# A front without queries, and a lag of two between gate and down products, in a gated cross-attention and mixture-of-experts layer on one core

## The chip, the cores and the metric

The kernel runs on one NeuronCore of a Trainium2 chip. The metric is the device time of one execution in microseconds. A core has five engines that run side by side, each through its own list of instructions: PE (TensorE, matrix products), DVE (VectorE), ACT (ScalarE), POOL (GpSimd) and SP (SyncE, which here only issues transfers). They wait for each other by semaphores.

## The reference, cut to what matters

```python
# x: (4, 256, 256), ctx: (4, 256, 64)
p    = layernorm(x)                                    # no gamma
kv   = ctx @ W_k.T + b_k
out  = einsum('bij,bjd->bid', p, kv)                   # queries
sim  = einsum('bid,bjd->bij', out, kv) / 16
sim  = (sim - mean) * rsqrt(var + 1e-6) * ln_gamma + ln_beta
x    = x + tanh(g_xattn) * softmax(sim)
h    = layernorm(x)                                    # 1024 tokens
s    = sigmoid(h @ gate_weight.T)                      # 16 experts, 4 groups
# two best groups by s + bias, four best experts of these, weights s/sum * 2.5
out  = sum_e w[t,e] * (silu(h @ gate_w[e].T) * (h @ up_w[e].T)) @ down_w[e].T
out += (silu(h @ sh_gate.T) * (h @ sh_up.T)) @ sh_down.T
x    = x + tanh(g_ffn) * out
```

## The kernel before

**Batches, halves, steps.** The 1024 tokens lie in 8 tiles of 128, two to a batch, four to a half of 512. Every expert is computed for every token and weighted with zero where it wasn't chosen. The shared expert counts as two of 128 columns, so each half has NF = 18 steps, 36 in all; step k is expert k of the first half, or k - 18 of the second. Precision comes from splitting: each fp32 operand becomes a high part (fp32r) and the rest as a low part, and three products stand for one (high times high, high times low, low times high).

**A step.** PE does the gate product (6 of 512 columns, L782), the up product (6 of 512) and, for the step before (lag of one), the down product (12 of 256, L826, L828, L834) into accumulators in PSUM banks 4 and 5 (first half) or 6 and 7. ACT takes the silu of the gate (L386), and makes the high parts of weights two steps ahead (high_gu) and of the down weights one ahead (high_d, both L327). POOL subtracts to get the low parts (L284). DVE multiplies by the expert's weight per token (L535, from a row that is broadcast by a transfer), then by up: act_hi (L553), the same product in fp32 (L556), and act_lo, the difference (L561). The first two routed experts, steps 2 and 3 (WEIGHTED_LAST), get their weight last, because the routing is late then: step 2's row comes by transposes on PE (first_row, L769), step 3's by the transfer. Steps 18 and 19 are shared again.

**What waits for what.** gate(k) waits for act_done of step k - 2 (L804), up(k) for actlo_done of k - 2 (L813), down(k - 1) for the parts of k - 1 (L822, L830).

**The front.** For each batch: statistics of x (L458 to L464), the power -1/2 on POOL (L278), the normalised x on DVE or ACT, its transposes on PE (L712), the context's projections kv and kvT (L700, L705), the query product (L721), the similarity (L729), its statistics, centring (L487), scaling (L495), maximum (L499), exponential on ACT (L363), residual (L514), statistics of the new x, hidden rows (L470), their transposes and high and low parts (L368, L524). Batches 0 and 1 are done before the steps; all four similarities are made before step 0 and batches 2 and 3 finish on DVE between steps 2 and 12. Products of zeros (keep_warm, L852) fill PE's waits.

**The routing.** route (L752) makes the logits transposed, logitT is copied by ACT, route_back (L760) transposes them, DVE adds the parts (L571), ACT takes an exponential (L378), and DVE does score_groups, rank_groups, mask_groups and pick_experts (L573 to L627): some 40 small instructions with waits between them. The order of all engines is written out by hand; each_step names which pieces come after which step. In before the routing of the first half is spread: scores ahead of step 0's parts, ranks after step 0, picks after step 1.

**Loads.** SP issues x in four pieces, then the weights of eight steps (384 KB each), later one slice and one row a step. ACT's queue issues the context, the vectors and the router's weights.

## Time and profile before

| | us |
|---|---|
| median of 3 runs | 195.62 |
| lowest, highest | 194.97, 199.32 |
| the profiled execution's own time | 194.61 |
| its span, first to last instruction | 192.8 |
| PE busy | 183.1 (95%) |
| DVE busy | 147.1 (76%) |
| ACT busy | 81.2 (42%) |
| POOL busy | 83.0 (43%) |

The span is what the trace covers; 1.8 us of the execution's time lie around it. A busy engine is one with an instruction in flight. Products are pipelined, so a row of a product can be longer than the distance to the next. The start of a row and the distance between starts say more than its length.

### The profile page before, as it was taken

The numbers are of one execution on the slowest core, as the hardware profiler recorded it, in microseconds if no ns is written. First come the engines' busy times: TensorE is split into PE (matmuls) and PEld (weight loads), VectorE is DVE, ScalarE is ACT, GpSimd is POOL, SyncE is SP. The second block draws the span as 40 slices with busy tenths as digits, with TensorE's granted clock in tenths as the row PEclk, the third lists the DMA queues.
The fourth block names the chain that finished last, engine by engine and source line by source line (L and its number), as shares of the span: only waits on it lengthen the run. The fifth ranks groups of instructions, "written<-read, shape, count | busy, mean of one in ns | idle before, by whom it ended". The sixth has DMA issues, their size and how long they took to land.

```text
span 192.8 us, 3265 instructions
## 1 busy us (share of the span) xinstructions
PE 183.1 (95%) x1003; PEld 151.9 (79%) x1003; DVE 147.1 (76%) x332; ACT 81.2 (42%) x160; POOL 83.0 (43%) x101
## 2 busy tenths in 40 slices
PE   6999799969899999999999989999999999999993
PEld 5665457858788888888788868888888888888882
DVE  1759988989899699998469999885666665566664
ACT  2449725523248833435457333434334343433220
POOL 2352162822841755553345543454444555444410
PEclk9999999999999999999999999999999999999999
DMA  5967200002785555541221000312211221221403
GB/s 145 344 212 217 76 0 0 0 0 57 235 205 183 150 141 163 161 139 58 54 54 54 0 3 9 109 57 74 80 60 54 54 54 60 74 78 60 143 20 112
DMA packets 10297, 18.08 MB, mean 94 GB/s; under 512 B 1773, under 2 KB 3821, under 8 KB 10286
## 3 DMA queue, kind: packets, MB, share of 16 engines
q1 hardware_dynamic: 9504, 17.11, 29.4%
q10 hardware_dynamic: 782, 0.83, 1.8%
q8 instruction: 6, 0.10, 0.2%
q14 instruction: 5, 0.04, 0.1%
HBM read 16.82 MB, written 1.11 MB: 93 GB/s over the span
## 4 chain that ended last, share of the span: by engine, by line
PE 67%; DVE 20%; DMA 6%; issue 2%; POOL 1%; ACT 1%; DVEq 0%; SPq 0%; POOLq 0%
PE bank L782 41%; PE bank L834 8%; PE bank L826 7%; PE bank L828 7%; DMA xs<-x_in 3%; DVE act_hi L553 2%; DVE bank L556 2%; DVE act_lo L561 2%; DMA w_row<-weight_rows 2%; DVE stats L458 1%; POOL rstd L278 1%; PE bank L712 1%; DMA weight_rows<-w_blk 1%; DVE beats L597 1%; PE bank L752 1%
## 5 line engine op out<-in xcount | busy, mean ns | idle before, releaser
L284 POOL TENSOR_TENSOR w_lo<-w_raw,w_hi 128x256 fp32r<-128x256 f32 (+1 forms) x72 | 72.4, 1024 | 76.7 <-ACT w_hi L327 75.6
L327 ACT CAST w_hi<-w_raw 128x256 fp32r<-128x256 f32 (+2 forms) x72 | 36.5, 513 | 56.4 <-PE bank L834 30.6
L782 PE MATMUL bank<-hT_hi,w_hi 128*128 128x512 f32 x142 | 56.5, 398 | 0.0
L782 PE MATMUL bank<-hT_lo,w_hi 128*128 128x512 f32 x142 | 56.0, 395 | 0.0
L782 PE MATMUL bank<-hT_hi,w_lo 128*128 128x512 f32 x142 | 44.7, 396 | 0.0
L535 DVE TENSOR_TENSOR weighted<-bank,w_row 128x512 f32<-128x512 f32 x30 | 20.7, 691 | 25.6 <-ACT bank L386 24.5
L826 PE MATMUL bank<-w_hi,act_hi 128*128 128x256 f32 x144 | 36.0, 283 | 1.8 <-DVE act_hi L553 1.8
L828 PE MATMUL bank<-w_lo,act_hi 128*128 128x256 f32 x144 | 35.8, 281 | 0.0
L782 PEld LDWEIGHTS bank<-hT_hi,w_lo 128*128 128x128 f32 x142 | 26.7, 188 | 6.3
L782 PEld LDWEIGHTS bank<-hT_hi,w_hi 128*128 128x128 f32 x142 | 26.8, 189 | 5.1
L826 PEld LDWEIGHTS bank<-w_hi,act_hi 128*128 128x128 f32 x144 | 27.2, 189 | 4.3 <-issue 2.8
L782 PEld LDWEIGHTS bank<-hT_lo,w_hi 128*128 128x128 f32 x142 | 26.8, 189 | 4.8
L386 ACT ACTIVATE bank<-bank 128x512 f32<-128x512 f32 x30 | 17.5, 582 | 26.4 <-PE bank L782 26.4
L828 PEld LDWEIGHTS bank<-w_lo,act_hi 128*128 128x128 f32 x144 | 27.2, 189 | 1.4
L561 DVE TENSOR_TENSOR act_lo<-bank,act_hi 128x512 fp32r<-128x512 f32 (+1 forms) x37 | 25.0, 677 | 3.6
L553 DVE TENSOR_TENSOR act_hi<-bank,weighted 128x512 fp32r<-128x512 f32 (+1 forms) x36 | 24.2, 675 | 2.8 <-DVE weighted L535 0.9
L834 PE MATMUL bank<-w_hi,act_lo 128*128 128x256 f32 x144 | 23.8, 287 | 1.0 <-DVE act_lo L561 0.7
L556 DVE TENSOR_TENSOR bank<-bank,weighted 128x512 f32<-128x512 f32 (+1 forms) x36 | 24.2, 675 | 0.0
L834 PEld LDWEIGHTS bank<-w_hi,act_lo 128*128 128x128 f32 x144 | 19.7, 190 | 2.2 <-DVE act_lo L561 2.2
L278 POOL TENSOR_TENSOR rstd<-var_eps,half_neg 128x2 f32<-128x2 f32 x12 | 8.7, 721 | 20.5 <-DVE var_eps L464 20.4
L852 PE MATMUL bank<-zeros 128*128 128x512 f32 x25 | 9.1, 508 | 1.5 <-DVE zeros L636 1.5
L852 PEld LDWEIGHTS bank<-zeros 128*128 128x128 f32 x25 | 5.6, 243 | 3.6 <-DVE zeros L636 1.5
(100 smaller groups left out, 133.2 us busy)
## 6 DMA issues: line engine op xcount, KB each, us to landing
w_row<-weight_rows SPq DMA_DIRECT2D x31, 256.0 KB, 3.2
w_raw<-w_in SPq DMA_DIRECT2D x18, 384.0 KB, 3.9
xs<-x_in SPq DMA_DIRECT2D x4, 256.0 KB, 5.9
out<-x SPq DMA_DIRECT2D x2, 256.0 KB, 3.5
cw<-ctxw_in ACTq DMA_DIRECT2D x1, 276.2 KB
vec<-vecs_in ACTq DMA_DIRECT2D x1, 265.0 KB, 5.6
out<-x SPq DMA_DIRECT2D x2, 128.0 KB, 1.8
out<-x ACTq DMA_DIRECT2D x2, 128.0 KB, 1.8
```

The lines of the kernel that those rows point to most:

```text
L284: nc.gpsimd.tensor_tensor(w_lo[:, par, cols], w_raw[:, bass.ds(n, 1), cols].rearrange("p o c -> p (o c)"), w_hi[:, par, cols].bitcast(F32) ...
L327: nc.scalar.copy(w_hi[:, par, cols], w_raw[:, bass.ds(n, 1), cols].rearrange("p o c -> p (o c)"))\
L386: nc.scalar.activation(gate_ps[par][:, :] if routed else weighted[:, par, :], gate_ps[par][:, :], ACT.Silu).then_inc(silu_done, 1)
L535: nc.vector.tensor_tensor(weighted[:, par, :], gate_ps[par][:, :], w_row[:, par, :], ALU.mult)\
L553: nc.vector.tensor_tensor(act_hi[:, par, toks], row[:, toks], weighted[:, par, toks], ALU.mult)\
L556: nc.vector.tensor_tensor(up_ps[par][:, toks], row[:, toks], weighted[:, par, toks], ALU.mult)\
L561: nc.vector.tensor_tensor(act_lo[:, par, toks], up_ps[par][:, toks], act_hi[:, par, toks].bitcast(F32), ALU.subtract).then_inc(actlo_done, 1)
L782: last = nc.tensor.matmul(dst, w[:, par, w0 + c * P:w0 + (c + 1) * P], m, start=i == 0, stop=i == len(parts) - 1, skip_group_check=True)
L826: nc.tensor.matmul(acc, act_hi[:, par, own], w_hi[:, par, rows], start=start and t % 2 == 0, stop=False, skip_group_check=True)
L828: nc.tensor.matmul(acc, act_hi[:, par, own], w_lo[:, par, rows], start=False, stop=False, skip_group_check=True)
L834: last = nc.tensor.matmul(acc, act_lo[:, par, own], w_hi[:, par, rows], start=False, stop=True, skip_group_check=True)
L852: last = nc.tensor.matmul(spare[:, :], zeros[:, 0:P], zeros[:], start=True, stop=True)
```

## The change

**Front.** The queries go. With the augmented context c (64 columns and a one), similarity is x c' M c, where M is the square of the key weights. So: squared() makes W'W (65x65) from W with its bias as a 65th column; the context of each batch is centred over its positions (times 256, so that no division is needed), which makes the similarity's row means zero; offset(b) is a product of one column that becomes the 65th column of the batch's square; projected(b) gives u (65x256); gathered(b) gives r (65x256) from context rows and x transposed, which now comes ready from the host as a fifth array; similarity(b) is r times u. Normalising x falls away, since the layer norm after it removes scale and mean: only the epsilon is corrected, by row_eps from x's variance. For batches 0 and 1 a second product with u times minus gamma (similarity_gamma) gives the scaled logits; ACT multiplies them by the root, and one DVE instruction adds minus beta and takes the minimum. Batches 2 and 3 keep scaling, logits and maximum on DVE.

**Loads.** SP's queue takes nearly all, in the order of need; ACT's has the key weights and the context rows of batch 0.

**Lag of two.** down(k - 2) stands in step k. Activation parts and down weights have three buffers. gate(k) waits for the weighting of k - 2 (weighted_done, or the silu where there is none) instead of act_done. In steps 2 and 3 DVE splits: weighted_late(k) inside the step, late_parts(k) later. The loops are unrolled.

**Moved.** The low parts of down weights are made for step k, not k + 1. Steps 0 and 1 are done by batches: gate and up for batch 0 of both before hidden(1). Similarities 2 and 3 stand among them. All of the first routing stands after step 1 on DVE; the router's exponential on ACT is after step 1 too.

```diff
 def each_step(eng, step, between):
-    straight(0, NF + 2)
-    loop(NF + 2, 2 * NF - 2)
-    straight(2 * NF - 2, 2 * NF)
+    for k in range(2 * NF):
+        step(k, k % 2)
+        for piece in between.get(k, ()):
+            piece()
 # SP
-            for b in range(B):
-                sp.dma_start(xs[...], x_v[...]).then_inc(x_in[b], 16)
-            ahead = 8
-            for n in range(ahead):
...
+            load_context(0, 1, cT0_in)
+            load_xT(0)
+            sp.dma_start(gamma_key[:], ...).then_inc(gamma_in, 16)
+            load_x(0)
+            load_context(1, 2, cT1_in)
+            load_xT(1)
+            load_rows(1, 2, rows1_in)
+            load_x(1)
+            sp.dma_start(vec[:], ...).then_inc(vec_in, 16)
+            load_slice(0, 0)
+            load_slice(1, 1)
+            load_context(2, B, cT_in)
+            load_xT(2)
+            load_xT(3)
+            load_rows(2, B, rows_in)
+            sp.dma_start(gw[:], ...).then_inc(gw_in, 16)
+            load_x(2)
+            load_x(3)
 # PE
             def gate_up(k, par, half):
                 pe.wait_ge(hi_gu, k + 1)
-                    pe.wait_ge(act_done, k - 1)
+                if k >= 2:
+                    if shared_or_late(k - 2):
+                        pe.wait_ge(silu_done, k - 1)
+                    else:
+                        pe.wait_ge(weighted_done, weighted_count(k - 2))
...
             def step(k, par):
-                if first == 1:
-                    pe.wait_ge(score_ready, 1)
-                    down(k - 1, 1 - par, int(first - 1 >= NF), first - 1 in (0, NF))
+                gate_up(k, par, k // NF)
+                if k >= 2:
+                    if k % NF == 2:
+                        pe.wait_ge(score_ready, k // NF + 1)
+                    down(k - 2)
 # ACT
-            table_change = {6: ..., 15: lambda: logit_exp(1)}
+            table_change = {7: lambda: (softmax_exp(2), softmax_exp(3)), 16: lambda: logit_exp(1)}
 # DVE
+            def sim_logits_negative(b):
+                for i, t in enumerate(tiles(b)):
+                    dve.wait_ge(scaled_read, 2 * b + i + 1)
+                    nc.vector.tensor_tensor_reduce(logit[:, t, :], scaled[:, t, :], beta_neg[:], 1.0, BIG, ALU.add, ALU.min,
+                                                   neg_max[:, t:t + 1]).then_inc(max_ready[b], 1)
...
             each_step(dve, step, {
-                0: [rank_groups, mask_groups],
-                1: [lambda: pick_experts(0)],
-                2: [lambda: sim_stats(3), lambda: sim_centre(3)],
...
+                1: [lambda: add_logits(0), lambda: score_groups(0), rank_groups, mask_groups, lambda: pick_experts(0)],
+                2: [lambda: sim_stats(2), lambda: sim_scale(2)],
+                3: [lambda: late_parts(2), lambda: x_stats(3), lambda: sim_stats(3), lambda: late_parts(3)],
+                4: [lambda: sim_scale(3)],
+                5: [lambda: sim_logits(2, 5)],
+                6: [lambda: sim_logits(3, 6)],
...
```

DVE's list around the first routing before: scores, then step 0's three parts, then the ranks (L593 on).

```order
L583 TENSOR_TENSOR pairs<-choice 128x16
L584 TENSOR_REDUCE gscore<-pairs 128x16
L553 TENSOR_TENSOR act_hi<-bank,weighted 128x512
L556 TENSOR_TENSOR bank<-bank,weighted 128x512
L561 TENSOR_TENSOR act_lo<-bank,act_hi 128x512
L593 TENSOR_TENSOR beats<-gscore 128x64
L594 TENSOR_TENSOR ties<-gscore 128x64
```

The same place of the changed kernel: the end of the routing (w_blk is what SP writes out for the row transfers), then step 2's and 3's late weighting (L588), batch 2's statistics and the late parts of step 2.

```order
L696 TENSOR_TENSOR w_tok<-pick_w,w_rec 128x4x16
L700 STREAM_TRANSPOSE w_blk<-w_tok 128x64
L588 TENSOR_TENSOR weighted<-bank,weighted 128x512
L488 BN_STATS stats<-bank 128x6 x2
L491 BN_AGGR meanvar<-stats 128x2 x2
L524 TENSOR_TENSOR var_eps<-meanvar,row_eps 128x2
L530 TENSOR_TENSOR scaled<-bank,vec 128x256 x2
L588 TENSOR_TENSOR weighted<-bank,weighted 128x512
L603 TENSOR_TENSOR act_hi<-bank,weighted 128x512
L604 TENSOR_TENSOR weighted<-bank,weighted 128x512
L606 TENSOR_TENSOR act_lo<-weighted,act_hi 128x512
```

The parts of steps 0 and 1 stand ahead of the whole routing now, and the parts of step 2 behind it and behind batch 2's statistics.

PE's list around the first early products before: zero products, both batches' hidden transposes (L712), the gate of batch 0, then the route.

```order
L852 MATMUL bank<-zeros 128x512 x6
L712 MATMUL bank<-ident,ln 128x128 x8
L795 MATMUL bank<-hT_hi,w_hi 128x256 x2
L795 MATMUL bank<-hT_hi,w_lo 128x256 x2
L795 MATMUL bank<-hT_lo,w_hi 128x256 x2
L752 MATMUL bank<-hT_hi,gw_parts 32x512 x2
```

And of the changed kernel, from early_up(1, 0) to the route (L873); L826 is the hidden transposes of batch 1, L840 a similarity, L804 a projected context.

```order
L916 MATMUL bank<-hT_lo,w_hi 128x256 x2
L826 MATMUL bank<-ident,hid 128x128 x4
L789 MATMUL bank<-ctx_sum,square 65x1
L840 MATMUL bank<-uT,rT 128x256 x2
L804 MATMUL bank<-cT_mid,square 65x256
L916 MATMUL bank<-hT_hi,w_hi 128x256 x2
L916 MATMUL bank<-hT_hi,w_lo 128x256 x2
L916 MATMUL bank<-hT_lo,w_hi 128x256 x2
L873 MATMUL bank<-hT_hi,gw_parts 32x512 x2
```

The transposes of batch 1 come behind four products with batch 0 (L916), and a similarity and a projection stand between them and the route.

## Rows read from the trace of the kernel before

**Rows 1.** The page: busy shares; granted clock of PE in 40 slices.

```profile
PE 183.1 (95%) x1003; PEld 151.9 (79%) x1003; DVE 147.1 (76%) x332; ACT 81.2 (42%) x160; POOL 83.0 (43%) x101
...
PEclk9999999999999999999999999999999999999999
```

**Rows 2.** Waits of PE: who waited for whom, us in total, times, longest.

```profile
PE bank L826 <- DVE act_hi L553: 1.8, 2, 1.4
...
PE bank L834 <- DVE act_lo L561: 0.7, 1, 0.7
```

**Rows 3.** The chain that ended last: start us, us, what.

```profile
61.51 2.79 PE bank L782 x12
...
65.73 2.79 PE bank L782 x12
...
97.45 3.02 PE bank L782 x12
...
115.94 2.79 PE bank L782 x12
```

**Rows 4.** Timeline of DVE, front: start us, us, instruction [idle before].

```profile
5.25 0.75 DVE L458 BATCH_NORM_STATS2 stats<-xs 128x6 f32<-128x256 f32 x2 [3.85 <-DMA xs<-x_in]
...
9.55 0.74 DVE L458 BATCH_NORM_STATS2 stats<-xs 128x6 f32<-128x256 f32 x2
...
10.62 0.75 DVE L458 BATCH_NORM_STATS2 stats<-xs 128x6 f32<-128x256 f32 x2
...
13.81 0.76 DVE L458 BATCH_NORM_STATS2 stats<-bank 128x6 f32<-128x256 f32 x2 [2.02 <-PE bank L729]
...
27.46 0.69 DVE L524 TENSOR_TENSOR hT_lo<-bank,hT_hi 128x512 fp32r<-128x512 f32 x1 [0.15 <-ACT hT_hi L368]
```

**Rows 5.** Timelines of PE in five stretches, the last with its weight loads.

```profile
4.62 1.41 PE L852 MATMUL bank<-zeros 128*128 128x512 f32 x3
...
7.81 0.97 PE L852 MATMUL bank<-zeros 128*128 128x512 f32 x3
...
10.53 1.08 PE L721 MATMUL bank<-lnT,kv 128*64 128x256 f32 x4
...
57.12 0.40 PE L782 MATMUL bank<-hT_hi,w_hi 128*128 128x512 f32 x1
...
188.38 0.30 PEld L834 LDWEIGHTS bank<-w_hi,act_lo 128*128 128x128 f32 x2 [0.20 <-DVE act_lo L561]
```

**Rows 6.** Groups by line: count | busy us, mean ns | idle before.

```profile
L284 POOL TENSOR_TENSOR w_lo<-w_raw,w_hi 128x256 fp32r<-128x256 f32 (+1 forms) x72 | 72.4, 1024 | 76.7 <-ACT w_hi L327 75.6
...
L278 POOL TENSOR_TENSOR rstd<-var_eps,half_neg 128x2 f32<-128x2 f32 x12 | 8.7, 721 | 20.5 <-DVE var_eps L464 20.4
...
L363 ACT ACTIVATE prob<-logit,neg_max 128x256 f32<-128x256 f32 x8 | 4.0, 500 | 1.3 <-DVE neg_max L499 1.3
...
L514 DVE SCALAR_TENSOR_TENSOR x<-prob,attn_scale,xs 128x256 f32<-128x256 f32 x7 | 3.1, 480 | 0.1
...
L470 DVE TENSOR_SCALAR ln<-x,meanvar,rstd 128x256 f32<-128x256 f32 x8 | 2.8, 406 | 0.3 <-POOL rstd L278 0.3
```

**Rows 7.** Timeline around the first routing, ACT and DVE.

```profile
31.45 0.26 ACT L378 ACTIVATE inv_score<-route_logit 128x64 f32<-128x64 f32 x1 [0.92 <-DVE route_logit L571]
...
31.73 1.28 ACT L386 ACT_TABLE_LOAD   x1
31.74 0.20 DVE L577 TENSOR_SCALAR inv_score<-inv_score 128x64 f32<-128x64 f32 x1 [0.32 <-ACT inv_score L378]
...
36.46 1.20 DVE L596 TENSOR_TENSOR ties<-ties,before 128x64 f32<-128x64 f32 x1
...
43.68 0.24 DVE L626 STREAM_TRANSPOSE w_blk<-w_tok 128x64 f32<-128x64 f32 x1
```

**Rows 8.** The chain: the weights' way out and the first row's way back.

```profile
43.96 2.06 DMA weight_rows<-w_blk
46.03 3.21 DMA w_row<-weight_rows
```

More of the change, by code:

```diff
@@ new lines, in _ @@
+                9: [lambda: x1_stats(2), lambda: residual(3)],
+                10: [lambda: x1_stats(3)],
+                11: [lambda: normalise(2, 2, 7, x1, hid, hid_ready)],
+                12: [lambda: normalise(2, 3, 8, x1, hid, hid_ready)],
+                13: [lambda: hidden_low(2), lambda: hidden_low(3)],
+                15: [lambda: add_logits(1)],
+                16: [lambda: score_groups(1), rank_groups],
+                17: [mask_groups, lambda: pick_experts(1)],
+                NF + 1: [lambda: result(0)],
@@ L883, in _ @@
-            keep_warm(6, bank[5])
-            hidden(0)
+            keep_warm(3, bank[7], P)
+            pe.wait_ge(zeros_ready, 2)
+            keep_warm(4, bank[7])
+            squared()
+            keep_warm(3, bank[7])
+            offset(0)
+            keep_warm(2, bank[7])
+            gathered(0)
+            projected(0)
+            offset(1)
+            keep_warm(1, bank[7])
+            similarity(0)
+            gathered(1)
+            projected(1)
+            similarity_gamma(0)
@@ new lines, in _ @@
+            similarity(1)
+            similarity_gamma(1)
+            pe.wait_ge(var_ready, 1)
+            keep_warm(3, bank[0])
+            gathered(2)
+            gathered(3)
+            keep_warm(7, bank[0])
+            pe.wait_ge(ident_ready, 2)
+            pe.wait_ge(r_ready, 2)
+            hidden(0)
+            keep_warm(2, bank[0])
+            early_gate(0, 0)
+            early_up(0, 0)
+            offset(2)
+            early_gate(1, 0)
+            projected(2)
+            early_up(1, 0)
@@ L885, in _ @@
+            pe.wait_ge(u_ready, 2)
             hidden(1)
-            first_gate(0)
-            route(0)
+            offset(3)
+            similarity(2)
+            projected(3)
             each_step(pe, step, {
-                12: [lambda: hidden(2), lambda: hidden(3)],
-                13: [lambda: route(1)],
-                14: [lambda: route_back(1)],
-            })
-            down(2 * NF - 1, 1, 1, False, spans(2 * NF - 1))
+                0: [lambda: similarity(3)],
+                13: [lambda: hidden(2), lambda: hidden(3)],
+                14: [lambda: route(1)],
+                15: [lambda: route_back(1)],
+            })
```

680 lines of the change are left out of this document (371 added, 309 removed).

## The prediction

> **What bounds the kernel now.** I read the page's busy shares first [rows 1]: PE is busy for 95% of the span, DVE for 76%, at a granted clock of 9 tenths or more in each of the 40 slices. So only two things can shorten the span: PE starts its useful products sooner, or it waits less between them. The waits of PE [rows 2] are small: 1.8 and 0.7 us on DVE's two activation parts. The chain of waits then shows where time is lost between products [rows 3]. From the gate of one step (61.51) to that of the next (65.73) go 4.22 us, and PE is full there: 36 steps make 152 us that this change leaves alone. From 97.45 to 115.94 stand four steps, 18.49 us for 16.88 of products: 1.6 us are lost, and the chain runs through DVE there. At the end PE waits 0.20 us for a last act_lo (188.38) [rows 5]. The rest is the front: DVE gets its first x at 5.25, reads the first similarity at 13.81 and ends the low part of batch 0's hidden rows (28.15, from 27.46) before PE can finish a first expert product [rows 4].
>
> **The change, part by part.** I take before's own trace as the clock of both.
>
> Front to the first similarity. Normalisation, transposes and queries of batch 0 (5.25 to 12.6) go. In their place: a 65x65 square of the weights, a one-column offset, two products of context rows with x transposed (gathered), one with the centred context (projected). No row shows the landing of the first small context load. It is bounded by the 2.06 us of a 16 KB write [rows 8] after an issue at 0.75, so 2.8, and by x's 5.25; I take 3.1, near the lower end, since it is the first and small. With DVE's sums, the square's copy and the offset, gathered(0) starts at 5.5. A pair of fp32 products of 256 columns takes 1.08 [rows 5], one takes 0.54, a copy 0.4 to 0.5: 5.5 + 1.08 + 0.54 + 0.45 + 1.08 = 8.65. The zero products run at 0.43 us each up to 5.2 and at 0.23 at 7.8 (three from 4.62, three from 7.81; a group is two distances and one length long) [rows 5], i.e. PE is at its lower level of 1.2 GHz first; as gathered(0) falls in between, I add 0.45: the first similarity is read at 9.1 instead of 13.81.
>
> The same place by the Trainium skill: "DMA: Bandwidth & Descriptors", section "Issuing engines are not separate DMA queues", says that transfers issued by SP and by ACT run on the same DMA engines and interleave. The trace agrees in that x, issued first, took until 5.25 while the ACT queue's context load was in flight. By that rule one queue in order of need is worth nothing by itself, only the smaller first load is; it gives rival 3.
>
> DVE's chain from there. One mean and variance of two tiles takes 1.07 (9.55 to 10.62) [rows 4], 1.15 with its last instruction's end, and a root on POOL 0.72 [rows 6]. So 9.1 + 1.15 + 0.75 + 0.5 (ACT scales a tile; the 0.50 of an exponential row) + 0.1 of hand-overs = 11.6. The new add-and-minimum instruction (tensor_tensor_reduce) is in no row: at least one pass over a tile (0.48, as L514) [rows 6], at most two (0.96). I take 0.55, nearest to the one pass. Then DVE does, back to back: minimum 1.1, statistics 1.15, scale 0.4, residual 0.9 (2 x 0.48 less overlap), statistics 1.15, minimum 1.1, normalise 0.75 (2 x 0.41 less overlap), scale 0.4, residual 0.9, statistics 1.15, low part 0.65: 9.65. Low part of batch 0 ready at 21.3 instead of 28.15. The two exponentials (0.50 each) lie under DVE's work; so do x loads 2 and 3.
>
> PE from 21.3. A third of the early gate (0.23), then early up(0) 0.70, offset 0.1, gate(1) 0.70, projected 0.54, up(1) 0.70: 24.3. Only now hidden(1), 0.6, though its rows are ready at about 22.0: the early products stand ahead of it. Offset 0.1, similarity(2) 1.08, projected(3) 0.54: 26.6; gate(0) of batch 1 0.70 and route 0.94: 28.3; then up 0.70, similarity(3) 1.08, gate(1), route_back and up(1) 1.76: 31.8. Nothing of the 6.9 us won has been lost so far except 3.3 us of fp32 products that before stood in the front.
>
> The routing chain. It decides the next 25 us. ACT: logitT 0.57 (28.9), table load 1.28, silu 0.60: 30.8. DVE now does steps 0 and 1 whole (three passes of 128x512, 0.69 each as the hT_lo pass [rows 4], 2.05 with a little overlap): 34.9; add_logits 0.3, exponential 0.26: 35.5. In before the routing's pieces (score_groups, rank_groups, mask_groups, pick_experts) run from 31.74 to the end of w_blk at 43.92, 12.18 us, with the parts of two steps between them, 2.1 each: 7.95 of their own [rows 7]. That includes stretched rows such as 1.20 for a multiply of 64 elements beside others of its size at 0.20, while POOL subtracts. I take 7.95: 43.45, only 0.5 us ahead of before's 43.92. Here most of the front's gain stops. Behind it in DVE's queue: weighted_late(2) 0.65, statistics and scaling of batch 2 1.95, weighted_late(3) 0.65, the parts of step 2 2.0, statistics 2.25, the parts of step 3 2.6, step 4 2.7: 56.25. PE waits in this stretch for weights_ready at first_row, for act_hi(2) and for act_lo(4), ahead of up(6). The row loads (2.06 + 3.21 [rows 8]) end at 48.7 and are covered by DVE's queue. So up(6) runs 56.3 to 57.7. In before gate(6) starts at 57.12 [rows 5] and up(6) ends at 59.9, with one down product (1.42) more behind it. Lead: 59.9 - 57.7 - 1.42 = 0.8 us.
>
> What the bound on this term is: if POOL never holds DVE, the routing costs 1.8 less (the 1.20 row alone has 1.0 over a row of its size, and I allow nearly as much for its neighbours) and the lead is 2.6; if the minimum takes 0.96 and a load lands 1 us late the lead is 0.8 - 1.6 - 1.0 with nothing hidden, -1.8.
>
> Lag of two. From step 7 on gate(k+2) needs weighted(k), up(k+2) act_lo(k). With DVE's 2.7 us a step (four passes of 0.69) against PE's 4.22 it catches up by step 9. In the middle (97.45 to 115.94) the second routing puts about 4.7 us into step 16 and 3.3 to 4.9 into 17, from the same 7.95 and the 1.6 lost there. A lag of two gives up(18) 7.0 us after up(16) ends, against the 2.8 us of before, and act_lo(17) comes 4.8 to 5.5 us after up(17): covered, so 1.6 us come back. At the end down(34) lies between up(35) and down(35): 0.3 back, the 0.20 wait and the 0.1 around it. Its price: high_gu(9) on ACT stands behind exponentials that wait for DVE's neg_max of batch 3 (65.2), so it ends at 66.9, and PE wants it at 67.1. I cost it at nothing; the cover is 0.2 us. Two more table loads (1.28 each [rows 7]) on ACT lie under DVE's steps.
>
> Sum: 0.8 + 1.6 + 0.3 = 2.7 us. The profiled execution took 194.61 us (span 192.8, 1.8 around it), so 191.9 us, span 190.1. The median of the runs shown is 195.62, 1.0 above the profiled one; such a spread stays inside my range.
>
> **Rivals.**
> 1. The routing chain is not held by POOL, and front and chain run to the short ends: lead 2.6 instead of 0.8, 190.1, or 189.0 with context and x loads 1 us sooner. For it: most of the routing's rows took 0.2 us, so the stretched ones are few and fall by chance. Against: POOL's subtractions, 72 at 1.02 us [rows 6], fill 2.0 of each 4.2 us in either kernel.
> 2. The lag does not do what it says: DVE, with all routing in step 1 and both late steps in step 3, is the bound, and a wait on DVE takes the place of the old one. Already in my sum up to step 6; if it goes on to step 16, the 1.6 us of the middle stay lost and ACT's 0.2 us cover too: 193.7.
> 3. Loads late. If order in a queue does not hold, the first context load lands with x at 5.25 instead of 3.1: 2.1 later at every point, of which the sum hides nothing: 194.0. The minimum instruction at two passes ends close by (193.5).
> 4. Slower. PE waits 1.6 us (19.4 to 21.0) for the low part, after zero products and waits of its own. If it falls to 1.2 GHz there and stays low through the 10.5 us up to 31.8, these take twice as long, route ends 7.0 later and all of DVE's chain with it, and the last products up to 10.5 later: 198.9 to 202.4, some 200.5. It decides for slower from 7.6 us of products at the low level on. For it: the first 3.7 us and more ran at half rate [rows 5]. Against: an idle gap of 1.4 us ahead of an L826 product [rows 2] was followed by steps at the full pace of 4.22, that of the 2.4 GHz level. The Trainium skill, "TensorE: Matmul & The Clock Gate", section "What's actually happening", says that the default state is the throttled one and activity releases it; by it a front with thinner activity could rise later, and the zero products here are fewer at a time.
>
> **How the numbers follow.** My forecast (190.5 to 193.2, likeliest 191.9) has 0.46; rival 1 0.20; rival 2 0.12; rival 3 0.15; rival 4 0.07. The range leaves out rival 4 and the far end of rival 1: 188.5 to 195.5. A change of over 2%, about what a measurement of this kernel can tell from none, is a time below 191.7 or above 199.5. Below: rival 1 and nearly half of my forecast, 0.20 + 0.22 = 0.42. Above: 0.07. Between: 0.51.
>
> **What would show it.** After's trace should have the first statistics of a similarity at about 9.1, the first hT_lo ending near 21.3, PE waiting there some 1.6 us; w_blk ending at 43.0 to 43.9; waits of PE on w_tok, act_hi and act_lo between 40 and 57 of 4 us or more in sum; gates 4.22 us apart from step 7 to the end, with none missing around the second routing. I am wrong if w_blk ends before 41 (then rival 1), if gates are further apart than 4.3 between steps 7 and 18 (rival 2), or if zero products or early products are seen at the 0.43 pitch after 8 us (rival 4).

## The result, and the profile after

The changed kernel takes 197.64 us (median of 5 runs, 196.42 to 203.82), the kernel before, run between them, 196.21 (194.97 to 199.40). The ratio is 1.011, interval 1.008 to 1.014: slower by about 1%. The prediction was 191.9, with 188.5 to 195.5: wrong in size and in sign. Both kernels have executions 3 to 7 us longer than their others, which the ratio leaves out; some profiles below are of such executions, so I compare stretches of them and not their ends.

The profiled execution took 196.42 us (span 194.8), 1.8 more than that of before (194.61). PE's busy sum is 0.9 smaller (182.2 for 183.1 us, [rows 1]), so all that was added is waiting. The page:

```profile
PE 182.2 (94%) x1007; PEld 152.4 (78%) x1007; DVE 146.7 (75%) x337; ACT 78.5 (40%) x162; POOL 81.3 (42%) x98
...
DVE  3689922888999979999976999796666656666653
...
PEclk9999999997899999999999999999999999999999
```

DVE is at nine tenths or more in nine of the ten slices from 49 to 97 us (a slice is 4.87), and the granted clock has a dent in the tenth and eleventh. The waits of PE, which answer to [rows 2]; columns: who waited for whom, us in total, times, longest:

```profile
PE bank L890 <- DVE scaled L530: 3.0, 1, 3.0
PE bank L826 <- DVE hid L509: 2.4, 3, 1.6
PE bank L916 <- DVE hT_lo L582: 1.1, 1, 1.1
```

The old waits on act_hi and act_lo (1.8 and 0.7) are gone. The wait of 3.0 is new and the longest of these, and the prediction did not have it. It is first_row (L890): it sits inside the gate of step 4 and writes bank 6, which held the similarities of batch 2. So it waits for the routing weights and for DVE's read of those similarities, which the change puts behind the routing. PE's timeline there, then the windows of 3 us around it (length, busy time of each engine with its count, granted clock, DMA):

```profile
43.63 0.40 PE L903 MATMUL bank<-hT_hi,w_hi 128*128 128x512 f32 x1
46.98 1.09 PE L890 MATMUL bank<-ident,w_tok 128*128 128x128 f32 x4 [2.95 <-DVE scaled L530]
47.72 0.78 PE L903 MATMUL bank<-hT_lo,w_hi 128*128 128x512 f32 x1
48.29 1.05 PE L903 MATMUL bank<-hT_hi,w_lo 128*128 128x512 f32 x2
...
50.17 0.39 PE L903 MATMUL bank<-hT_lo,w_hi 128*128 128x512 f32 x1
```
```profile
44.00:47.00 3.00, 0.05 (x2) 0.05 (x1) 2.90 (x11) 0.00 (x0) 0.75 (x2) 0.90 0.07 11
47.00:50.00 3.00, 3.00 (x10) 2.57 (x11) 2.22 (x4) 0.58 (x1) 1.85 (x2) 0.53 0.65 199
```

The weights were ready at 44.1; PE starts at 46.98, and after the gap the clock granted averages 0.53, close to the level of 1.2 GHz, until about 50. DVE's own chain loses less than PE: it stands idle for 0.74 us, until first_row's row is there for act_hi(2):

```profile
48.18 0.69 DVE L603 TENSOR_TENSOR act_hi<-bank,weighted 128x512 fp32r<-128x512 f32 x1 [0.74 <-PE bank L890]
```

DVE's front, which answers to [rows 4], and then a stretch behind step 7 in which ACT stands 2.40 us on the maximum of batch 3, loads a table, and so lets DVE stand 1.15 us for the silu of step 8:

```profile
9.75 0.76 DVE L488 BATCH_NORM_STATS2 stats<-bank 128x6 f32<-128x256 f32 x2 [0.27 <-PE bank L840]
...
15.05 1.92 DVE L570 SCALAR_TENSOR_TENSOR x<-prob,attn_scale,xs 128x256 f32<-128x256 f32 x2
...
20.20 0.88 DVE L570 SCALAR_TENSOR_TENSOR x<-prob,attn_scale,xs 128x256 f32<-128x256 f32 x2
...
22.19 0.68 DVE L582 TENSOR_TENSOR hT_lo<-bank,hT_hi 128x512 fp32r<-128x512 f32 x1
...
71.99 0.69 DVE L615 TENSOR_TENSOR weighted<-bank,w_row 128x512 f32<-128x512 f32 x1 [1.15 <-ACT bank L429]
```
```profile
68.15 0.51 ACT L406 ACTIVATE prob<-logit,neg_max 128x256 f32<-128x256 f32 x1 [2.40 <-DVE neg_max L544]
...
70.08 1.28 ACT L429 ACT_TABLE_LOAD   x1
71.38 0.58 ACT L429 ACTIVATE bank<-bank 128x512 f32<-128x512 f32 x1
```

The gain in front is real: the first low part ends at 22.87, where it was 28.15. It is lost behind it. From step 15 to the end the chain of waits reads as predicted, which answers to [rows 3]. Around the second routing a step takes 4.22 us again; the first one here is longer by route_back's products (0.36, L881), the second by 0.2:

```profile
99.36 2.80 PE bank L903 x12
103.12 0.48 PE bank L972 x4
103.60 0.36 PE bank L881 x4
103.96 3.00 PE bank L903 x12
107.92 0.48 PE bank L972 x4
108.40 2.80 PE bank L903 x12
111.67 0.12 PE bank L964
112.14 0.48 PE bank L972 x4
112.62 2.80 PE bank L903 x12
```

### The profile page after: what moved, and what is told of

The parts are those of the page before. It is cut to its first block, busy times and chain, and to the rows that moved or that the text cites. A ratio compares the mean times of both kernels' runs of the same rounds, so it can differ in the third digit from the quotient of the medians.

```text
span 194.8 us, 2988 instructions
## 1 busy us (share of the span) xinstructions
PE 182.2 (94%) x1007; PEld 152.4 (78%) x1007; DVE 146.7 (75%) x337; ACT 78.5 (40%) x162; POOL 81.3 (42%) x98
## 4 chain that ended last, share of the span: by engine, by line
PE 61%; DVE 27%; issue 4%; ACT 3%; DMA 2%; POOL 1%; SPq 1%; DVEq 0%; ACTq 0%
PE bank L903 36%; PE bank L972 6%; PE bank L964 6%; PE bank L966 6%; DVE stats L488 3%; DVE act_hi L627 3%; DVE bank L630 3%; DVE x L570 2%; DVE act_lo L635 2%; DMA xs<-x_in 2%; PE bank L916 2%; DVE weighted L615 2%; DVE hid L509 1%; DVE meanvar L491 1%; PE bank L840 1%
## 5 line engine op out<-in xcount | busy, mean ns | idle before, releaser
L323 POOL TENSOR_TENSOR w_lo<-w_raw,w_hi 128x512 fp32r<-128x512 f32 x36 | 46.7, 1297 | 77.3 <-ACT w_hi L367 76.5
L964 PE MATMUL bank<-d_hi,act_hi 128*128 128x256 f32 x144 | 35.9, 282 | 0.7 <-ACT inv_score L421 0.7
L966 PE MATMUL bank<-d_lo,act_hi 128*128 128x256 f32 x144 | 35.8, 281 | 0.0
L367 ACT CAST w_hi<-w_raw 128x512 fp32r<-128x512 f32 x36 | 22.2, 618 | 25.7 <-PE bank L903 23.6
L964 PEld LDWEIGHTS bank<-d_hi,act_hi 128*128 128x128 f32 x144 | 27.2, 189 | 2.6 <-ACT inv_score L421 1.1
L328 POOL TENSOR_TENSOR d_lo<-w_raw,d_hi 128x256 fp32r<-128x256 f32 x36 | 27.2, 756 | 4.5 <-ACT d_hi L372 4.5
L966 PEld LDWEIGHTS bank<-d_lo,act_hi 128*128 128x128 f32 x144 | 27.1, 188 | 1.5
L630 DVE TENSOR_TENSOR bank<-bank,weighted 128x512 f32<-128x512 f32 (+1 forms) x35 | 23.5, 674 | 0.0
L972 PE MATMUL bank<-d_hi,act_lo 128*128 128x256 f32 x144 | 23.2, 282 | 0.0
L972 PEld LDWEIGHTS bank<-d_hi,act_lo 128*128 128x128 f32 x144 | 19.8, 190 | 0.0
L372 ACT CAST d_hi<-w_raw 128x256 fp32r<-128x256 f32 x36 | 14.4, 401 | 0.0
```

Source lines behind the costliest of these rows:

```text
L323: nc.gpsimd.tensor_tensor(w_lo[:, k % 2, :], w_raw[:, k % NF, 0:GU], w_hi[:, k % 2, :].bitcast(F32), ALU.subtract).then_inc(lo_gu, 1)
L328: nc.gpsimd.tensor_tensor(d_lo[:, k % 3, :], w_raw[:, k % NF, GU:WCOL], d_hi[:, k % 3, :].bitcast(F32), ALU.subtract).then_inc(lo_d, 1)
L367: nc.scalar.copy(w_hi[:, k % 2, :], w_raw[:, k % NF, 0:GU]).then_inc(hi_gu, 1)
L630: nc.vector.tensor_tensor(up[:, toks], up[:, toks], weighted[:, par, toks], ALU.mult)\
L964: nc.tensor.matmul(acc, act_hi[:, par, own], d_hi[:, par, :], start=start and t % 2 == 0, stop=False, skip_group_check=True)
L966: nc.tensor.matmul(acc, act_hi[:, par, own], d_lo[:, par, :], start=False, stop=False, skip_group_check=True)
```

## The experiments

The front differs so much from one execution to the next that I read each profile from one mark: the end of w_blk (the routing weights), to the start of the last down product. In the table, all from profiles but the last column (lowest, median and highest time of all runs, us; the kernel before had medians of 194.8 to 194.9 beside them, but 196.21 beside the changed kernel, so times are compared with the changed kernel's by their ratios to the kernel before):

```
                 hT_lo(0)  w_blk  last down  distance   time
changed kernel     22.87   44.38   191.06     146.68   196.42 197.64 203.82
e1_batch2_early    24.62   52.80   197.83     145.03   196.31 202.46 205.34
e2_batches23_early 29.03   51.90   195.07     143.17   195.28 200.41 202.72
e3_softmax_step8   26.21   53.03   198.86     145.83   196.87 202.56 204.22
e4_warm_in_wait    24.64   46.75   193.00     146.25   196.32 197.20 198.32
e5_pool_later      24.08   45.58   192.00     146.42   197.19 197.40 203.61
e6_route_early     23.30   48.58   194.97     146.39   197.03 200.93 201.63
e7_two             23.77   51.99   194.75     142.76   194.17 197.20 200.79
e8_all             23.76   49.31   191.69     142.38   196.98 197.20 197.76
e9_warm_front      24.09   45.58   191.99     146.41   196.40 196.79 197.32
e10_best           23.56   46.34   188.56     142.22   193.34 194.00 196.08
e11_best_route     23.59   46.05   188.66     142.61   193.48 194.96 196.80
e14_warm_guard     23.29   44.78   187.93     143.15   193.26 195.19 200.98
e12_guard          23.12   44.74   185.71     140.97   191.08 191.63 193.61
e13_guard_masked   23.38   44.28   185.02     140.74   190.38 191.57 192.60
e15_gate_wait_undone 23.52 45.02   192.56     147.54   197.90 198.47 199.75
```

**first_row's wait, and DVE's order.** e1 moves two calls of DVE ahead of the routing, e2 the other two as well:

```
             hidden_low(1)
+            sim_stats(2)
+            sim_scale(2)
+            x_stats(3)
+            sim_stats(3)
...
-                2: [lambda: sim_stats(2), lambda: sim_scale(2)],
```

> Only the place of two steps on DVE changes: the statistics and the scaling of similarities of batch 2 stand right after hidden_low(1), ahead of the routing, and no longer behind it. Theory A (first_row's PE wait is for DVE's scaling of batch 2, since first_row writes the bank that held those similarities, and the clock falls in the gap of 2.95 us): first_row starts within 0.3 us of weights_ready, at about 44.2 where it was at 46.98; the granted clock stays at 1.00 there; DVE's chain behind the routing is 1.85 us shorter, gate(7) starts at 59.2 to 59.8 where it was 61.34; the time is 1.2 to 2.0 us under the changed kernel's, some 195. Theory B (DVE's work in steps 0 to 7 is the bound by its sum, whatever waits for what): DVE's work is only moved into the 4.5 us in which it was idle ahead of silu(0), which B too counts as a gain of up to 1.85 us, but first_row's gap alone gives nothing, so the clock shows no effect at the end. Theory C (the loss is in steps 7 to 13, by softmax_exp and Pool): the lead at step 7 is used up before step 14 and the time stays within 0.4 us of 197.6.

> As the run before it, and the statistics of x and of the similarities of batch 3 are put ahead of the routing as well (another 1.1 us of DVE's work behind the routing gone). Theory A: gate(7) at 57.5 to 58.7, the time 2.3 to 3.5 us under the changed kernel's, some 194.5. The part of it that is DVE's work rather than first_row's wait is the difference to the run before: about 1.0 us if DVE bounds steps 0 to 7, 0 if only first_row's wait and the clock mattered. Theory C: both runs stay within 0.4 us of 197.6.

first_row now starts with the weights. PE in e1:

```profile
52.58 0.65 PE L891 MATMUL bank<-ident,w_tok 128*128 128x128 f32 x4 [1.28 <-DVE w_tok L696]
52.99 0.48 PE L904 MATMUL bank<-hT_lo,w_hi 128*128 128x512 f32 x1
```

It takes 0.65 us at full clock, and the distance is 1.65 us shorter; in e2 3.51. By the time alone e1 can't tell theory A from B, since both expected some 1.85 us. DVE's rows can. From the end of w_blk to the end of act_lo(4) the changed kernel needs 13.80 us and e1 12.17. The statistics and the scaling of batch 2 (1.76) are gone from there, and so is DVE's idle 0.74 for first_row; 0.26 waiting for the row of step 3 and 0.5 more of Pool's holds have come in. So the second wait of first_row, for all its 2.95 us on PE, costs the chain about 0.74 us, and the larger part of the gain is DVE's work (theory B). In e2 the stretch takes 10.29 us: 2.30 of work less and no hold by Pool (1.5 in e1), but DVE now stands 2.19 us on the row of step 3, which its queue had covered before. The wait stays in every kernel that has this edit; in e12:

```profile
50.33 0.69 DVE L607 TENSOR_TENSOR act_hi<-w_row,weighted 128x512 fp32r<-128x512 f32 x1 [2.23 <-DMA w_row<-weight_rows]
```

The two transfers of the weights (2.03 and 3.48 us in e12's chain) are the next bound there, and no run takes it on. That w_blk itself ended late in e1 and e2 no theory had said.

**The clock in that gap.** e4 fills it:

```
             def first_row():
+                pe.wait_ge(silu_done, 4)
+                keep_warm(12, bank[1])
                 pe.wait_ge(weights_ready, 1)
```

> Twelve products with zeros are put ahead of first_row's waits, in PE's gap of 2.95 us at 44.0 to 46.98; nothing else changes, first_row still waits for DVE's scaling of batch 2. It takes the fall of the clock from the wait. If the fall is the loss (theory D: PE at a granted 0.53 from 47 to 50 made act_hi and all behind it late): granted clock 0.9 or more in 47 to 50, first_row 0.65 us where it took 1.10, gate(7) earlier by about 1.5 us and the time 1.2 to 1.8 us lower. If DVE's order is the loss (theory A): the clock is mended just the same, but DVE is behind anyway, act_hi(2) starts 0.4 to 0.5 us earlier at most, and the time is 0 to 0.5 us lower. If it was the clock's own doing and not the gap's, the clock falls again in spite of the products.

The clock stayed up (1.00 for the span), first_row took 0.62, DVE's idle time for it fell from 0.74 to 0.28, and the distance fell by 0.43. That is theory A's figure. The fall at 47 us followed from the wait and is more than half of its price, but not the main loss.

**The exponentials.** e3 changes one number: `table_change = {8: ...}` for `{7: ...}`.

> The exponentials of softmax for batches 2 and 3 are given to ACT one step later (step 8 where it was 7), so that ACT no longer stands 2.4 us on DVE's maximum at 68.15 with high_gu(9) and silu(8) behind it. Theory C (this wait makes steps 7 to 13 lose 2.5 us): weighted(8) starts without the 1.15 us in which DVE was idle, and the time is 0.8 to 1.3 us under the changed kernel's. Theory A does not touch it: no change in gate(7), and at the end between 0 and 1.2 us, since DVE's maximum and weighting are on one chain. If the wait has only moved to another place (the silu of step 9), the time is the same within 0.3 us.

ACT waits for no maximum any more, weighted(8) follows act_lo(7) without a gap, and the distance is 0.85 us shorter: theory C holds with its lower figure.

**The front, from run to run.** The profile of e1 in windows of 5 us, PE alone (length, busy time and count, granted clock, DMA):

```profile
20.00:25.00 5.00, 2.30 (x11) 0.83 0.72 219
25.00:30.00 5.00, 5.00 (x22) 0.50 0.02 9
30.00:35.00 5.00, 5.00 (x18) 0.50 0.02 3
35.00:40.00 5.00, 5.00 (x29) 0.81 0.00 0
```

After the stretch with gaps for hid and hT_lo the clock falls to half, and w_blk ends at 52.8 for 44.4. The same fall stands in the profiles of e3, e6, e7 and e8, a shorter one in e5 (0.66 from 15 to 20), and none there in that of the changed kernel itself. e2 shows a second thing that the granted clock does not tell. Its timeline comes first, the same products in the changed kernel's under it:

```profile
18.27 1.91 PE L853 MATMUL bank<-uT_gamma,rT 65*128 65x256 f32 x4
19.63 1.84 PE L990 MATMUL bank<-zeros 128*128 128x512 f32 x3
21.27 3.19 PE L821 MATMUL bank<-xT,rows 128*65 128x256 f32 x8
```
```profile
12.87 1.10 PE L850 MATMUL bank<-uT_gamma,rT 65*128 65x256 f32 x4
13.62 1.06 PE L987 MATMUL bank<-zeros 128*128 128x512 f32 x3
14.51 1.89 PE L818 MATMUL bank<-xT,rows 128*65 128x256 f32 x8
```

Granted is 1.00 in both, yet e2's products run at half pace from the start to about 24 us; the changed kernel's doubled theirs at about 6, e1's at 9 to 10, e3's at 14. The Trainium skill, "TensorE: Matmul & The Clock Gate", section "What's actually happening", has the throttled state as the default that activity lifts; e2 agrees as far as its first 24 us go, with 1.91 us for four products that take 1.10 at the full pace. e9 tests whether it is PE's own gaps that decide:

```
-            keep_warm(4, bank[7])
+            keep_warm(8, bank[7])
             squared()
-            keep_warm(3, bank[7])
+            keep_warm(1, bank[7])
...
-            keep_warm(7, bank[0])
+            keep_warm(13, bank[0])
...
-            keep_warm(2, bank[0])
+            keep_warm(3, bank[0])
```

and eight short ones in early_gate(0,0) ahead of hT_lo's wait. In this kernel, e10 and e11 those eight write the second half of a bank whose first half is summing, and so spoil that sum (the output is off by a relative 0.17); they are read for their time alone. In e12 to e15 four long ones in a bank of their own stand there instead.

> Only products with zeros are added or moved on PE: eight in one piece at the start where it was four and three with a small product between, six more in the gap ahead of hidden(0), one more and eight short ones in the two gaps ahead of hT_hi and hT_lo, twelve ahead of first_row. In the profiles of the changed kernel and of the eight runs before, two things vary from run to run: when PE's pace doubles (a product of 256 columns goes from 0.48 to 0.26 us; at about 6 us in four of them, at 9 to 25 in five), and whether the granted clock falls to 0.50 between 22 and 37 us (in five of nine), after a stretch of 5 us with 2.2 to 3.6 us of products. Theory D (the gaps bring the fall, the start's mix the late rise): granted clock 1.00 throughout, pace doubled by 7 us, no run above 198, median 196.0 to 196.8. Theory G (the fall and the rise come by chance, whatever PE does): a third or more of the runs at 200 or above again, or the profile shows the fall.

All four runs were at clock 1.00 and within 0.9 us, and the median lies at the upper end of theory D's range. By its ratio (1.008, 1.005 to 1.011) e9 is not shown to be faster than the changed kernel (1.011, 1.008 to 1.014); what it changes is the spread. Of the 40 runs without these covers (the changed kernel and e1 to e8) 16 took more than 200 us and 15 had a granted clock under 0.98 over the span. Of the 54 with them (e9 to e15) one took more than 200 (200.98), and none had a clock under 0.988; in all seven profiles the pace doubled by about 7 us. Some of these kernels are faster for other reasons, so the clock is the better witness. So what PE does in the front has to do with the fall. Which gap does it is not shown, and the length of the gaps alone does not decide: from 20 to 25 us, both near full clock, e4 had only 2.16 us of products and no fall behind it, and e8 had 3.03 us and fell to 0.50.

**Pool and DVE.** e5 moves one call of Pool behind gw_parts:

```
             root(1, 1)
-            low_gu(1)
             root(2, 0)
...
+            low_gu(1)
             root(2, 1)
```

> Only Pool's order changes: low_gu(1), a subtraction of 1.28 us beside which DVE's two residual(0) operations took 1.92 us where the kernel before shows 0.88, is put later, ahead of the root of batch 1's second half. Theory E (Pool's subtraction holds DVE's operations that read two operands from SBUF): residual(0) takes 0.9 to 1.0 us, the first hT_lo is ready at about 21.8 to 21.9 where it was 22.87, and hidden(0) about 1 us earlier; at the end 0 to 1.0 us lower, nearer 0.3, because hidden(1) waits for other work. If it was not Pool (the operation by itself is slower here), residual(0) takes 1.9 us again and nothing moves.

residual(0) took 0.88, as expected for Pool. But the hold only moved: normalising, further down DVE's list, took 1.72 where it had taken 0.73, and hT_lo gained nothing. DVE in e5, and Pool's subtraction beside the second row:

```profile
16.31 0.88 DVE L570 SCALAR_TENSOR_TENSOR x<-prob,attn_scale,xs 128x256 f32<-128x256 f32 x2
...
19.31 1.72 DVE L509 TENSOR_SCALAR hid<-x,meanvar,rstd 128x256 f32<-128x256 f32 x2 [0.23 <-POOL rstd L318]
```
```profile
19.46 1.42 POOL L323 TENSOR_TENSOR w_lo<-w_raw,w_hi 128x512 fp32r<-128x512 f32 x1
```

**PE's order, and sums.** e6 sets hidden(1) ahead of the second early up:

```
             hidden(0)
             keep_warm(2, bank[0])
-            early_gate(0, 0)
-            early_up(0, 0)
             offset(2)
-            early_gate(1, 0)
+            early_gate(0, 0)
             projected(2)
-            early_up(1, 0)
+            early_up(0, 0)
+            offset(3)
+            early_gate(1, 0)
+            projected(3)
             pe.wait_ge(u_ready, 2)
             hidden(1)
+            early_up(1, 0)
```

e7 is e2 with e3, e8 is e2, e3, e5 and e6.

> PE's order in the front changes: the last products of up(0) and gate(1) and the early similarities, which stood ahead of hidden(1), are interleaved by halves so that hidden(1) starts when its operand is there (23.8) and not at 26.23; ACT copies the projections of batch 3 ahead of hidden(1)'s copy. Theory F (the routing starts late because hidden(1) stands behind early products): hidden(1) starts at 24.5 to 25.3, the routing ends 1.0 to 1.7 us earlier, at about 42.7 to 43.4, and as everything behind it hangs on the routing the time is 0.7 to 1.5 us lower. If DVE's chain from the hidden states of batch 1 is the bound anyway, the routing ends within 0.3 us of 44.38 and the time stays.

> Batches 2 and 3 ahead of the routing and the exponentials one step later together. If the two losses lie one behind the other (A in steps 0 to 7, C in steps 7 to 13), their gains add: 3.2 to 4.6 us under the changed kernel's. If a lead won ahead of step 7 is used up by DVE in steps 8 to 13, the sum is no more than the larger of the two alone.

> All four edits together: DVE's batches 2 and 3 ahead of the routing, the exponentials one step later, Pool's subtraction later, hidden(1) earlier. By the sum of the parts at their middle values (2.9 + 1.0 + 0.3 + 1.0) 5.2 us under the changed kernel's, about 192.4; if one bound hides the others, as DVE would from step 7 on, about 194.

e7's distance is 3.92 us shorter, near the sum of its parts (3.51 + 0.85). e8 adds to it 0.38. Its time stayed at 197.2 all the same, since the clock fell in the front. e6 says nothing by itself for the same reason; e11, below, gives the answer.

e10 is e2 (x_stats(3) one place earlier), e3 and e5 with the covers of the front (nine zero products ahead of hidden(0), none ahead of first_row), and on ACT:

```
-            high_gu(0)
             scale_rows(0)
+            high_gu(0)
             softmax_exp(0)
```

e11 is e10 with e6.

> The covers of the run before, and with them what the earlier runs showed to be worth something behind the routing: DVE's batches 2 and 3 ahead of the routing (x_stats(3) now in the idle time before hidden_low(1)), the exponentials one step later, Pool's low_gu(1) later, and on ACT scale_rows(0) ahead of high_gu(0), which stood on the first load of weights (landing between 10.5 and 12.9 us). From the end of w_blk to the last down product the changed kernel took 146.7 us, the runs with both edits 142.8 and 142.4. With w_blk's end at 44.0 to 45.5 that gives a last down at 186.8 to 188.3 and a time of 190.5 to 192.0, under the kernel before (194.9) by 1.5 to 2.3 per cent. If a cover is wrong and the clock falls in the front, w_blk ends at 49 or later and the time is 195 or more.

> The run before with PE's order in the front changed as well, so that hidden(1) does not stand behind the early products of the shared experts. At full clock this was not yet seen (the clock fell in both profiles that had it). If hidden(1) then starts when its operand is ready, w_blk ends 0.7 to 1.5 us earlier than in the run before and the time is 0.7 to 1.5 us lower. If DVE or the copies of ACT between bound it, the two are equal within 0.3 us; if the interleaving takes products from gaps that they filled, the clock falls in this one and not in the other.

e10 has w_blk at 46.34 and 194.00 us, ratio 0.997 (0.9945 to 1.000) to the kernel before: 2 us over the expected range. e11 has w_blk 0.29 us earlier and no better time, so hidden(1)'s place is worth next to nothing; theory F falls. Of e10's 2 us, 1.6 are a slip in my sum: from the start of the last down product to the execution's time lie 5.3 to 5.4 us in these profiles, and I had allowed 3.7. The distance itself came as expected (142.22). The rest is w_blk, 0.84 us past the latest I had taken, and its trace has a hold there, DVE and Pool in the same 3 us of the routing:

```profile
43.45 0.23 DVE L690 TENSOR_TENSOR picked<-masked,replaced 128x64 f32<-128x64 f32 x1
43.72 1.20 DVE L691 TENSOR_TENSOR pick_w<-picked,score 128x64 f32<-128x64 f32 x1
44.95 0.22 DVE L692 TENSOR_REDUCE w_sum<-pick_w 128x4 f32<-128x64 f32 x1
```
```profile
43.51 1.33 POOL L323 TENSOR_TENSOR w_lo<-w_raw,w_hi 128x512 fp32r<-128x512 f32 x1
44.80 0.71 POOL L328 TENSOR_TENSOR d_lo<-w_raw,d_hi 128x256 fp32r<-128x256 f32 x1
```

A product of 64 elements lasts until Pool's subtraction (43.51 to 44.84) is over. The same reads in steps 5 to 13 for logit (1.47 for two tiles), residual (1.92) and hid (1.25), in which the two take 0.88, 0.88 and 0.73 when alone. In e14 (on e9) and e12 (on e10), both with the covers in a bank of their own, Pool waits for DVE instead; e13 holds step 2 back too:

```
+            after_dve = {3: (weights_ready, 1), 4: (actlo_done, 4), 6: (logit_ready[2], 2), 7: (logit_ready[3], 2),
+                         9: (scale_ready[3], 1), 12: (hid_ready[2], 2), 13: (hid_ready[3], 2)}
             def step(k, par):
+                if k in after_dve:
+                    pool.wait_ge(*after_dve[k])
```

> The kernel with the covered gaps (e9_warm_front, 196.79 us; the covers now write a bank of their own), and in it Pool's subtractions of seven steps wait until DVE is through with the operations that read two operands from SBUF: in step 3 for the routing weights, in step 4 for late_parts(3), in steps 6 and 7 for logit, in step 9 for the attention scales, in steps 12 and 13 for hid. Theory E (Pool's subtraction holds such an operation until it is over): pick_w takes 0.23 us, logit 0.44 each, residual(2) 0.88 for two, hid 0.73 for two, DVE's chain from the routing to step 13 is 2.5 to 4.5 us shorter, and the time is 1.5 to 3.5 us under 196.8. Rival: the operations take as long as before whatever Pool does, and only Pool's results come later: the time is the same or up to 2 us longer, with PE waiting for w_lo.

> The kernel e10_best (194.0 us; covers moved to a bank of their own) with the same waits of Pool. Theory E: the routing ends 1.0 us earlier (pick_w 0.23 for 1.20), steps 5 to 13 are 2 to 3 us shorter as far as DVE bounds them, the time 190.5 to 192.5, under the kernel before (194.8) by 1.2 to 2.2 per cent. Rival: PE is the bound once DVE is less than 2 us too long, so that only 1 us is gained, 193; or Pool's work is late for the low parts of the weights and nothing is gained.

> The run before, with Pool's step 2 as well behind the routing weights, so that masked takes 0.23 us where it took 0.95. PE then waits about 0.6 us for w_lo of step 4, since it needs it right behind first_row. If DVE bounds until step 13, 0.5 to 0.8 us less than the run before; if PE's wait counts, the same or 0.5 us more.

Groups of DVE from 36 to 100 us, of the changed kernel and of e12 (count, busy us, mean ns, idle before):

```profile
L509 DVE TENSOR_SCALAR hid<-x,meanvar,rstd 128x256 f32<-128x256 f32 x4 | 2.5, 670 | 0.0
L538 DVE SCALAR_TENSOR_TENSOR logit<-scaled,rstd,vec 128x256 f32<-128x256 f32 x4 | 2.3, 624 | 0.0
L570 DVE SCALAR_TENSOR_TENSOR x<-prob,attn_scale,xs 128x256 f32<-128x256 f32 x4 | 2.2, 586 | 0.0
```
```profile
L574 DVE SCALAR_TENSOR_TENSOR x<-prob,attn_scale,xs 128x256 f32<-128x256 f32 x4 | 1.8, 478 | 0.0
L542 DVE SCALAR_TENSOR_TENSOR logit<-scaled,rstd,vec 128x256 f32<-128x256 f32 x4 | 1.7, 478 | 0.0
L513 DVE TENSOR_SCALAR hid<-x,meanvar,rstd 128x256 f32<-128x256 f32 x4 | 1.5, 405 | 0.0
```

With Pool out of the way the same instructions take nearly their own length. e14's distance is 3.26 us under e9's, and its median 1.6 (195.19 for 196.79). e12: 191.63 us, ratio 0.987 (0.983 to 0.991); e13: 191.57, ratio 0.985 (0.981 to 0.988). Both are faster than the kernel before by more than the noise, though by less than 2%. masked took 0.23 in e13 where it had taken 0.95. w_blk ends 0.46 us earlier and the distance is 0.2 shorter, but act_lo(2) was held instead (1.57 for 0.69), and by the medians the two kernels are equal.

**The gate's wait.** e15 is e9, with the covers in a bank of their own, and one line put back:

```
-                        pe.wait_ge(weighted_done, weighted_count(k - 2))
+                        pe.wait_ge(act_done, k - 1)
```

> e9_warm_front with one part of the change undone: a gate product of a routed expert waits again for DVE's exact activation product of the step two before (act_done) and not only for its weighting. DVE is the later engine in steps 4 to 13, and act_done comes 1.4 us behind weighted_done. If gates were ever released by the weighting there, each such step loses up to 1.4 us and the time is 1 to 5 us over 196.8; if PE is always later than both marks, because it stands on act_lo for up() and down() anyway, the time is the same within 0.3 us, and that part of the change was worth nothing.

The distance is 1.13 us longer and the median 1.7 (198.47 for 196.79); PE waits 2.3 us for DVE's L630 in three places. That part of the change does gain.

## Why the prediction was wrong

On the profiled execution the sum missed by 4.5 us (196.42 for 191.9). The lead at step 7 came out at -1.25 instead of 0.8 (gate(7) starts at 61.17 for 61.34 in the kernel before, with one down product of 1.42 more behind it): 2.0 us. From gate(7) to gate(15) went 38.03 us where e13, the quickest, needs 35.57: 2.5 us. From there to the end the promised 1.9 us came.

- **Lag of two.** The step that failed with the most weight is "With DVE's 2.7 us a step (four passes of 0.69) against PE's 4.22 it catches up by step 9". The 2.7 left out what else is in DVE's queue: logits, scales, residuals, statistics and hid take another 1.1 to 2.7 us in each of steps 5, 6 and 8 to 12, where a step has 1.5 to spare, in part because Pool stretches them. DVE was behind until step 13, and that is where the 2.5 us went. This is rival 2, which I stopped at step 6. e14 differs from e9 by Pool's waits and takes 36.02 us from gate(7) to gate(15) for 38.27: Pool's holds alone make up about 2.25 of it. For the second routing the step was right: gates 4.22 us apart from step 17 on, and the 1.6 us did come back.
- **high_gu(9)** was costed at nothing with a cover of 0.2 us. neg_max came at 68.1 for 65.2, the cover was gone, and e3 wins back 0.85. It is a part of the same 2.5 us, not added to it.
- **Front to the first low part** (predicted 21.3, was 22.87). "Residual 0.9" failed: it was 1.92, beside Pool's low_gu(1), and e5 has 0.88 without it. The first statistics (9.1, was 9.75) are the rest. The minimum instruction was costed too high: two took 0.77 (12.51 to 13.28), not 1.1. PE's 1.6 us wait came as 1.14.
- **PE from 21.3.** hidden(1) stood behind the early products as said, and route ended at 30.0 for 28.3, late by about what the front was.
- **The routing** was costed at 7.95 and took 7.0, so that w_blk ended only 0.93 late (44.38 for 43.45). The 1.8 us that I gave to Pool's holds as the bound of this term is the right size: 0.72 was seen here (masked), and 0.97 more in e10 (pick_w).
- **Behind the routing.** From w_blk to the end of act_lo(4) I had 12.8 us, and it took 13.80 (58.18 for 56.25). The prediction had PE wait at first_row for weights_ready alone. The code has a second wait on the line below, for DVE's scaling of batch 2: I read the queue of DVE but not who waits for each entry. That cost DVE 0.74 us, of which e4 wins back 0.43 through the clock. Pool's hold of act_lo(3) (1.72 for 0.69) cost 1.03. The other entries were costed 0.8 too high. The larger gains of e1 and e2 (1.65 and 3.51) are mostly of work that the prediction had counted in this place, and that can stand elsewhere.
- **Loads** (rival 3): the first weights landed between 10.5 and 12.9 us over nine profiles, and ACT stood on them ahead of scale_rows(0). The profiled execution was the earliest; that may be part of why the median lies 1.2 us above it.
- **The clock** (rival 4, 0.07) was under-weighed. It was no feature of the profiled front, but one of the five runs took 203.82 us at a clock of 0.955, and the profiles of e1, e3, e6, e7 and e8 show the fall, at 197.0 to 204.2 us, where 198.9 to 202.4 were priced. With PE's gaps covered no profile has it.

That e12 takes 191.6 us, the figure predicted for the changed kernel, is luck and no check on the sum: it has 4 us of DVE's work moved that the prediction had left behind the routing, and a new wait of 2.23 us for a row.

Not settled: why e10 to e14 vary by 2 us and more at a clock of 1.00 (e13: three runs at 190.4 to 190.8 and three at 192.3 to 192.6). I did not separate the late doubling of PE's pace from the place of the loads there.

## What to carry to other kernels

When a change moves work behind a long serial chain on one engine, list for each moved entry who waits for it, bank reuse included: a helper's second wait left PE idle for 2.95 us here. Then ask what that idle time costs the engine that is the bound: it was 0.74 us. Before calling an engine covered, add up all that stands in its queue in those steps, and keep Pool's long subtractions out of the moments in which DVE works on operands from SBUF. When work is moved out of a queue, look for what it had covered: a row's transfer was the next wait. Judge a front by several profiles: of the nine without covers only one had no late pace, no late load and no fall in the front, and it was the one of the changed kernel.

## What was not expected of the hardware

- A DVE operation with two operands from SBUF lasts until Pool's subtraction beside it ends, whatever its own size: 1.20 us for 64 elements (0.23 alone), 0.92 for two elements (0.23 alone). The normalising pass, with one tensor operand, was held as well (1.72 for 0.73); operations with an operand in PSUM kept their 0.69. Pool is held in its turn: beside DVE's late parts in e1 its subtractions took 1.73 us for 1.30 and 1.18 for 0.72. The Trainium skill, "SBUF — State Buffer", section "SBUF: two separate sides", has this as an exclusive lock of a port pair for the whole instruction, taken also by DVE's 2-port modes; the trace agrees.
- PE ran at half pace with a granted clock of 1.00 for the first 6 to 24 us, by the run: in these profiles the granted clock does not show the first rise, only the length of a product does.
- A gap of 2.95 us with no product was followed by a granted clock of 0.53 over the next 3 us; 12 products with zeros in it kept 1.00.
- Products with a start flag in one half of a bank disturb a sum that is still open in the other half: the output of e9, e10 and e11 was off by a relative 0.17, that of e12 to e15, with the products in another bank, was not.
